# Scatters of an expert stage paced by GELU chunks, one by one, instead of five to a tile

## The reference

```python
x = x + tanh(g_xattn[0]) * L0_xattn(layernorm(x), ctx, ...)
x = x + tanh(g_ffn[0])   * L0_ffn(layernorm(x), ...)      # the experts
x = x + tanh(g_xattn[1]) * L1_xattn(layernorm(x), ctx, ...)
x = x + tanh(g_ffn[1])   * L1_ffn(layernorm(x), ...)      # int8-like

# L0_ffn: router -> softmax -> top 2 of 8, weights renormalised
h = gelu(x @ w_fc[e] + b_fc[e])          # 128 -> 512, for each expert e
y = sum over the 2 chosen e of weight_e * (h @ w_proj[e] + b_proj[e])
```

## Time and profile before

| | |
|---|---|
| median of 3 runs | 817.15 us |
| lowest, highest | 816.35, 824.14 us |
| span of the profiled execution | 881.7 us |
| own time of the profiled execution | not given beside its span |
| TensorE busy in it | 708.1 us (80%) |
| VectorE busy | 710.4 us (81%) |
| ScalarE busy | 566.2 us (64%) |
| GpSimd busy | 585.0 us (66%) |
| mean granted TensorE clock | 0.900 of full |

### The profile page before, as it was taken

How to read it: one execution, slowest core, us unless ns; L and a number is a source line. 1 busy time by engine, 2 the same in 40 slices (tenths; PEclk the granted TensorE clock), 3 DMA queues, 4 the chain that set the end, 5 groups by cost and what they waited for, 6 DMA issues and landing times. The chain is left out here.

```text
span 881.7 us, 19709 instructions
## 1 busy us (share of the span) xinstructions
PE 708.1 (80%) x6550; PEld 550.0 (62%) x6550; DVE 710.4 (81%) x1855; ACT 566.2 (64%) x1172; POOL 585.0 (66%) x570
## 2 busy tenths in 40 slices
PE   6998999999998998699369978988984789476435
PEld 3776777777776776577247767877872567233134
DVE  4999988888888998489166757767876899889988
ACT  4666566767676664576046656666766787488756
POOL 4675588888887788677746544656555898188810
PEclk9999899999999999899769989999996999755759
DMA  8414532323232222757348778878775933000005
GB/s 241 137 38 141 109 129 66 134 68 131 96 104 80 91 97 103 256 169 227 115 144 266 225 205 252 253 249 256 232 235 174 353 98 108 15 1 0 1 24 169
DMA packets 95430, 127.69 MB, mean 145 GB/s; under 512 B 20529, under 2 KB 65153, under 8 KB 94305
## 3 DMA queue, kind: packets, MB, share of 16 engines
q1 hardware_dynamic: 85760, 108.00, 40.0%
q0 software_dynamic: 8672, 17.99, 5.9%
q10 hardware_dynamic: 896, 0.43, 0.2%
HBM read 82.76 MB, written 43.53 MB: 143 GB/s over the span
## 5 line engine op out<-in xcount | busy, mean ns | idle before, releaser
L590 POOL DMA_INDIRECT m_results<-a_probs,e_to x142 | 146.9, 1035 | 106.6 <-ACT a_probs L827 59.4
L614 POOL TENSOR_TENSOR a_probs<-a_probs,a_top 128x1024 f32<-128x1024 f32 x64 | 122.0, 1906 | 57.0 <-DVE a_top L1682 56.0
L805 ACT ACTIVATE room<-a_ps_s,e_bias 128x512 f32<-128x512 f32 (+1 forms) x160 | 102.0, 652 | 85.8 <-PE a_ps_s L1111 54.8
L571 POOL DMA_INDIRECT m_tokens_to<-r_rows,r_place x128 | 133.9, 1046 | 32.3 <-issue 32.1
L1702 DVE CAST e_hp<-room 128x512 fp32r<-128x512 f32 (+1 forms) x160 | 67.8, 424 | 78.7 <-remote 32.2
L722 ACT ACTIVATE a_probs_t<-a_ps_pt 128x512 f32<-128x512 f32 x128 | 69.8, 592 | 84.5 <-PE a_ps_pt L1011 84.1
L1704 DVE TENSOR_TENSOR e_hp<-room,e_hp 128x512 fp32r<-128x512 f32 (+1 forms) x160 | 102.8, 643 | 5.5
L1634 DVE TENSOR_TENSOR a_probs<-a_ps_s,a_mask 128x1024 f32<-128x1024 f32 x64 | 77.9, 1217 | 13.4 <-PE a_ps_s L892 7.5
L995 PEld LDWEIGHTS a_ps_o<-a_vals,a_probs_t 128*64 128x64 f32 x2048 | 69.3, 140 | 30.0 <-issue 29.0
L995 PE MATMUL a_ps_o<-a_vals,a_probs_t 128*64 128x18 f32 x2048 | 77.2, 214 | 8.2 <-issue 7.0
L1682 DVE TENSOR_REDUCE a_top<-a_probs 128x16 f32<-128x1024 f32 x64 | 77.2, 1206 | 0.1
(11 more groups left out here) (422 smaller groups left out, 1901.6 us busy)
## 6 DMA issues: line engine op xcount, KB each, us to landing
e_weights<-m_weights_to SPq DMA_DIRECT2D x80, 512.0 KB
m_weights_to<-r_parts SPq DMA_DIRECT2D x8, 1024.0 KB
room<-m_tokens_to SPq DMA_DIRECT2D x31, 264.0 KB
c_two<-m_results SPq DMA_DIRECT2D x3, 1536.0 KB, 10.8
a_ctx_in<-in_ctx_dram SPq DMA_DIRECT2D x17, 256.0 KB, 2.8
m_keys_t<-n_keys SPq DMA_DIRECT2D x16, 256.0 KB
m_values<-n_values SPq DMA_DIRECT2D x16, 256.0 KB
out_dram<-x_all SPq DMA_DIRECT2D x15, 256.0 KB, 2.4
```

The lines of the kernel that those rows point to most:

```text
L571: pool.indirect_dma_start(tokens_to, bass.IndirectOffsetOnAxis(ap=place[:, k, q:q + 1], axis=0), rows[:, c % RING, q % CT, k, :], None).th ...
L590: pool.indirect_dma_start(results, bass.IndirectOffsetOnAxis(ap=to[:, v, r:r + 1], axis=0), y[:, v, r], None).then_inc(returned[v], 16)
L614: pool.tensor_tensor(probs[:, j], probs[:, j], top[:, j].unsqueeze(2).broadcast_to([P, HEADS, SEQ]), ALU.subtract).then_inc(shifted, 1)
L805: act.activation(h[:, c, at], ps_h[c][:, at], ACT.Gelu_apprx_tanh, bias=bias[:, n % ROWS, c:c + 1]).then_inc(h_sb, 1)
```

## The change

- `PACE` goes. In its place, `chunks_before_scatter(i)` says how many GELU chunks must be done before scatter i may be issued: 24 + i for the first 60, and then so that the 150th comes with the last chunks (76 chunks for 90 scatters).
- `beside_products` waits before every scatter, on `h_sb` (a GELU done) instead of `h_ps` (a product done).
- The count starts behind the results of tile 1, at the sixteen row scatters, instead of at tile 0.
- `constants()` moves from before the row scatters to before the results of tile 22.

```diff
-PACE = 5
+PACED_FROM, PACED_EVENLY = 6 * CHUNKS, 60
+LAST_SCATTER_AT = ETILES * CHUNKS
...
+def chunks_before_scatter(i):
+
+    even = min(i, PACED_EVENLY)
+    scatters = 2 * CT + row_parts_before(ETILES) - row_parts_before(2)
+    return PACED_FROM + even + (i - even) * (LAST_SCATTER_AT - PACED_FROM - PACED_EVENLY) // (scatters - PACED_EVENLY)
...
         def beside_products():
             nonlocal paced
-            if paced >= 0 and paced % PACE == 0:
-                pool.wait_ge(h_ps, min(paced // PACE + 1, ETILES - 1) * CHUNKS + 1)
             if paced >= 0:
+                pool.wait_ge(h_sb, chunks_before_scatter(paced))
                 paced += 1
...
         powers(SUPERS - 1)
-        paced = 0
         return_results(0)
         last_ratio()
         return_results(1)
-        constants()
+        paced = 0
         for q in range(TILES - CT, TILES):
             send_rows(q)
         for n in range(2, ETILES):
+            if n == EARLY + LATE_FULL // 2:
+                constants()
             return_results(n)
```

## The result

The changed kernel takes 827.82 us, median of 4 runs (825.92 to 832.02), beside 819.05 us of the kernel before in the same comparison: ratio 1.0118, 95% interval 1.0074 to 1.0163. It is slower by 1.2%, and it lies above the range that was given. Over all comparisons the kernel before was executed about 70 times; all but two of these executions lie between 813 and 826 us, one took 3360.8 us at a granted clock of 0.18 and is left out of the comparisons, and the profile of 881.7 us shown ahead of the prediction is the other one.

What follows compares the result with a forecast made beforehand. The experts were taken to run at TensorE's pace, with GpSimd's scatters ending the stage. From the timed median 817.15 us, 0 for the early wait and −4 for the late stretch gave 813 us; range 782 to 826.

Steps and rivals of the forecast that it cites:

- (a), the early wait: Experts, tiles 7 to 9: pacing prevents the burst of 27 scatters; 29.1 us in the profile, 0 taken for timed runs.
- the base it stood on: Profile span 881.7 us against timed median 817.15; the 64.5 us between them were placed where engines idle, mainly the experts.
- The small stalls of the late stretch: TensorE over 18 late tiles: 109.0 us against 99.1 at its pace; the 9.9 us may vanish after the change.
- (b), the ring and the row scatters: Row scatters and results queued behind the new waits still land in time: cost 0, up to 3 us per tile otherwise.
- (c), the constants: 3.7 us of GpSimd memsets move before tile 22's results; they delay only scatters before, and are counted in (d), the late stretch.
- (d), the late stretch: From tile 20's last GELU GpSimd runs without a stop, 117.1 to 123.9 us against 125.0: gain 1 to 7.9, taken as 4.
- Rival 3: Expert end: GpSimd's tail becomes the end if triples take under 18.0 us; 2 to 9 us slower, up to 826; chance 0.18.

Runs made afterwards that it cites:

- second profile of before: The kernel before, unchanged, profiled once more: 819.89 us, span 818.2.
- without waits: The kernel before with all its paced waits removed, so scatters go as soon as their data is there: 820.17 us, ratio 1.0006.
- one pause: The kernel before with a single wait, at the 38th scatter for the transposes of tile 13's rows, in place of all paced ones: 822.96 us, ratio 1.0022.

## Why the prediction was wrong

The forecast was 813, the measured time 827.82. Its third rival was what happened, at a price above its upper end.

- **(a), the early wait, and the base it stood on.** Right for the timed runs: it gave 0 there. But the argument kept the other end alive, a stall of 29.1 us that "begins and ends with the burst", and gave 0.34 to it or a share of it. As far as the runs show that was a coincidence in one execution: runs four times as long bring no stall (110 scatters in the second profile of before, 114 without waits). The warning stood in the text, a profile 7.9% longer than the median of the timed runs (64.5 of 817.15), and should have thrown out every reading of the stall. The small stalls of the late stretch, 9.9 us, came from the same execution; in all clean profiles tiles 21 to 39 take 96.4 us, not 109.0.
- **(b), the ring and the row scatters.** Cost 0, as predicted: tile 2 to 12 got no longer.
- **(c), the constants.** Predicted hidden before, and counted in GpSimd's late stretch after. Shown: putting them back gave 4.1 us of tail.
- **(d), the late stretch. This is the term that failed.** The time that GpSimd needs for it was right to a tenth. From tile 20's last GELU,

```profile
489.85 0.69 ACT L813 ACTIVATE room<-a_ps_s,e_bias 128x512 f32<-128x512 f32 x1 [0.67 <-PE a_ps_s L1119]
```

  that is from 490.54, to the last scatter's end at 614.50 it is 124.0 us, where 90 × 1.335 + 3.7 = 123.9 was worked out. What was wrong is what it was set against: 125.0 us for the same stretch before, read from the disturbed execution. At TensorE's pace it is 96.4 + 9.1 + 6.0 + 1.0 − 0.2 = 112.3 us (tile 21 to 39, the last gated result, the tail, the last scatter itself, less the 0.2 from that GELU's end to tile 21's start at 490.33, which here comes first). The "gain of 1 to 7.9" is a loss of 11.7.
- **Rival 3** had the mechanism, its place and its condition: three tiles in less than 18.0 us; they take 96.4 / 6 = 16.1. Its price, 2 to 9 us, was mis-sized because it took 11.6 us from tile 39 to the last gated result and 16.5 for a triple, again from the first profile; the clean ones give 9.1 and 16.1, and 11.7 in place of 9. (Six triples at 16.5 are 99.0 and not 99.1; nothing hangs on it.)
- **Left out of every case:** the piece between tiles 12 and 13, 4.4 us shorter after in the pair of profiles compared. It works against the tail, but how much of it the timed runs have is not shown.

For the two profiles the sum is −4.4 − 0.8 + 11.7 = +6.5 us; the medians differ by 8.8. With the 10.2 us of before without waits in place of 12.3 it is −2.3 − 0.8 + 11.7 = +8.6. That is one more single profile, so the agreement with 8.8 is not proof.

What stays open is the cause of the 29 us in the first profile. No later execution that was profiled has it, so it could not be tried. The Trainium skill ("SBUF — State Buffer", SBUF: two separate sides) has only the port pair of VectorE and GpSimd contend among the engines; the runs agree in so far as, up to tile 13's load, a run of scatters (from 395 to 435 us in the second profile of before) leaves no idle time of over 1.06 us on ScalarE and 0.56 on TensorE.

## What to carry to other kernels

If one profile is several per cent longer than every timed run, take a second one before reading anything from it; here the most conspicuous thing in it was not part of the kernel. Work that an engine puts off must fit into its idle time later: GpSimd needs 1.335 us for a scatter and gets ten in 16.1 us, so it works off a backlog by only two scatters in that time, and what it can't work off comes out in full at the end. Pace only where a profile shows who is hurt, and count the tail that it leaves. A gain read from one pair of profiles (here 4.4 us at one load) is only believed once timed runs repeat it; one pause had most of it in its profile, and its timed runs were no faster.

## What was not expected of the hardware

- One profiled execution of the kernel before lost 29 us in one place where the engines were nearly idle, with the same program as the other executions (813 to 826 us).
- A wait of TensorE of 2.92 us on one load cost 4.4 us more than one of 1.32 us at the same place: 1.6 us are the wait, and a stretch at 1.2 GHz followed it (0.72 of the granted clock on average over 12 us). The length of the wait alone does not tell whether that comes: 1.2 GHz followed 1.89 us of idle time in one kernel, and did not follow 1.96 us in another.
